# Two of three score steps between the halves of a slot's projections, and the low queries' step last

## The reference

```
Q = query @ w_q.T;  K = ctx @ w_k.T;  V = ctx @ w_v.T        # split into 16 heads
scores = einsum('bhqd,bhkd->bhqk', Q, K) / sqrt(32)
attn = softmax(scores);  c = einsum('bhqk,bhkd->bhqd', attn, V)
z = c @ w_o.T + b_o + query
out = (z - mean(z)) * rsqrt(var(z) + eps) * gamma + beta
```

## Time and profile before

| | us |
|---|---|
| median of 3 runs | 531.98 (531.88 to 532.25) |
| the profiled execution | 532.36 |
| its span, first to last instruction | 530.4 |
| mean granted TensorE clock | 0.995 |

### The profile page before, as it was taken

The page is one execution under the profiler, slowest core; times in us unless marked ns, Lnnn a source line. Parts: engine busy times, 40 slices in busy tenths (PEclk is TensorE's granted clock), DMA queues, the critical chain, the costliest instruction groups (busy, mean ns, idle before and its releaser), DMA issues.

```text
span 530.4 us, 12625 instructions
## 1 busy us (share of the span) xinstructions
PE 520.6 (98%) x4522; PEld 373.1 (70%) x4522; DVE 425.5 (80%) x877; ACT 423.9 (80%) x794; POOL 447.5 (84%) x387
## 2 busy tenths in 40 slices
PE   8999999999999999999999999999999999999994
PEld 7765577777777777777777767777766777777563
DVE  7886768887887778787878887888788778877887
ACT  6657777888888888888888888888888888877783
POOL 1725867999999999999999999999999999977956
PEclk9999999999999999999999999999999999999998
DMA  8953422344334332443243324333433432222123
GB/s 291 272 147 97 122 85 84 106 125 125 90 112 131 126 104 93 133 130 104 86 134 121 110 92 130 109 117 103 126 100 108 125 126 64 74 75 87 44 83 120
DMA packets 56750, 61.12 MB, mean 115 GB/s; under 512 B 29168, under 2 KB 29168, under 8 KB 56688
## 3 DMA queue, kind: packets, MB, share of 16 engines
q1 hardware_dynamic: 56688, 60.32, 36.4%
HBM read 39.58 MB, written 16.78 MB: 106 GB/s over the span
## 4 chain that ended last, share of the span: by engine, by line
PE 94%; DVE 3%; ACT 2%; issue 1%; DMA 0%; SPq 0%; DVEq 0%
PE ps_q L440 53%; PE ps_s L399 12%; PE ps_s L372 8%; PE ps_o L446 6%; PE ps_q L299 5%; PE ps_s L383 3%; PE ps_o L299 3%; PE ps_s L299 2%; PE ps_s L306 1%; DVE stats L812 1%; DVE z L808 1%; DMA max_rows<-max_turned 0%; ACT inverse L572 0%; DVE y L826 0%; DVE q_lo L722 0%
## 5 line engine op out<-in xcount | busy, mean ns | idle before, releaser
L446 PE MATMUL ps_o<-wo_hi,c_lo 64*128 64x512 f32 x448 | 180.1, 402 | 0.0
L440 PE MATMUL ps_q<-x_hi,wq_lo 64*128 64x512 f32 x448 | 179.8, 401 | 0.2 <-issue 0.2
L446 PE MATMUL ps_o<-wo_hi,c_hi 64*128 64x512 f32 x448 | 173.7, 388 | 0.0
L440 PE MATMUL ps_q<-x_hi,wq_hi 64*128 64x512 f32 x448 | 173.7, 388 | 0.0
L446 PE MATMUL ps_o<-wo_lo,c_hi 64*128 64x512 f32 x448 | 173.4, 387 | 0.0
L440 PE MATMUL ps_q<-x_lo,wq_hi 64*128 64x512 f32 x448 | 173.2, 387 | 0.0
L440 PEld LDWEIGHTS ps_q<-x_hi,wq_lo 64*128 64x128 f32 x448 | 82.4, 184 | 58.0 <-DVE z L808 46.1
L945 POOL TENSOR_TENSOR c_lo<-c_raw,c_hi 128x512 fp32r<-128x512 f32 x63 | 81.8, 1298 | 41.7 <-ACT c_hi L529 41.7
L969 POOL TENSOR_TENSOR y<-y,beta_row 128x512 f32<-128x512 f32 x59 | 103.9, 1760 | 4.6
L440 PEld LDWEIGHTS ps_q<-x_hi,wq_hi 64*128 64x128 f32 x448 | 82.4, 184 | 14.9
L440 PEld LDWEIGHTS ps_q<-x_lo,wq_hi 64*128 64x128 f32 x448 | 82.7, 185 | 12.6
(11 more groups left out here) (111 smaller groups left out, 1085.5 us busy)
## 6 DMA issues: line engine op xcount, KB each, us to landing
xT_raw<-in_xT SPq DMA_DIRECT2D x64, 256.0 KB, 3.0
x_raw<-in_x SPq DMA_DIRECT2D x64, 256.0 KB, 2.8
out<-y SPq DMA_DIRECT2D x64, 256.0 KB, 2.0
max_rows<-max_turned SPq DMA_DIRECT2D x128, 16.0 KB
ctx_raw<-in_ctxT SPq DMA_DIRECT2D x4, 256.0 KB, 5.1
wk_raw<-in_wkT SPq DMA_DIRECT2D x4, 256.0 KB, 5.3
wq_raw<-in_wqT SPq DMA_DIRECT2D x4, 256.0 KB, 6.0
wv_raw<-in_wvT SPq DMA_DIRECT2D x4, 256.0 KB, 6.7
```

The costliest lines, as they stand in the source:

```text
L440: return nc.tensor.matmul(ps_q[:, 0, :], w[l][half, k, dims], x_[r][half, qc % 2, k, :], start=(half is lower and k == 0 and step == 0), s ...
L446: return nc.tensor.matmul(ps_o[:, 0, :], cx[l][half, k, tile], wo[r][half, k, :], start=(half is upper and k == 0 and step == 0), stop=(ha ...
```

## The change

Of the three steps of a slot's scores, steps 0 and 1 now stand between the halves of `project_both` in the loop, and step 2 alone behind the second half; before it was step 0 between and steps 1 and 2 behind. The table of passes has its last two entries swapped, for every call of `score`: step 1 is now high keys by high queries, and step 2 high keys by low queries. The waits ahead of step 0 are as they were.

```diff
@@ -364,7 +364,7 @@
                     wait(pe, c_raw_done, n - 2)
-                passes = ((kbd_lo, q_hi), (kbd_hi, q_lo), (kbd_hi, q_hi))
+                passes = ((kbd_lo, q_hi), (kbd_hi, q_hi), (kbd_hi, q_lo))
                 for step in steps:
                     lhs, rhs = passes[step]
                     for pair in range(2):
@@ -494,9 +494,9 @@
             for t in range(OUT_LAG, SLOTS - 1):
                 project_both(t + 1, t - OUT_LAG, False)
                 subtract_max(t - 2)
-                score(t, range(1))
+                score(t, range(2))
                 project_both(t + 1, t - OUT_LAG, True)
-                score(t, range(1, 3))
+                score(t, range(2, 3))
                 combine_values(t - 2)
```

## The result

The changed kernel takes 538.5 us in the median against 532.04 for the one before, a ratio of 1.0118 (95% interval 1.0107 to 1.013): 6.5 us slower, where no change was forecast. Its profiled execution took 537.88 us with a span of 535.9, 5.5 us over the one before in both. The clock is no part of it, 0.996 against 0.995.

The account below looks back on a forecast made before the run. The prediction took TensorE's own steps, 7.62 us per slot over 56 slots, to bound the kernel. All terms were 0, so the 531.98 us median gave a forecast of 532.0 us, no change, with a range of 530.9 to 533.5.

Parts of the forecast that it names:

- The bound: Loop slot: 7.62 us as a sum of TensorE's own steps, none held by another engine.
- the 0.84 in front of L440: Slot start: the weight load's listed wait for z is the time of combine_values itself, 0.84 each, 46.1 us in total.
- Rival 3: Start of each slot: z or q_raw arrives after combine_values, TensorE stands; up to 12.7 us, 544.7; chance 0.03.
- The moved step: Between the halves: a score step costs 0.23 there as at the end; 0, bounded at 0.6 us either way.
- the swapped order: Score passes: kbd_hi x q_lo last releases nothing, since score() still waits for q_lo_done ahead of step 0; 0.
- Rival 1: Seams between the halves settle differently: +1.3 us (533.3), chance 0.08, or -1.2 us (530.8), chance 0.09.
- ACT: Query copies and q_hi shift 0.23 into 0.24 of idle time; log_sums slips 0 to 0.02; 0, bounded at 1.1 us.
- Rival 2: ACT's slip reaches c_raw once q_hi ends later than 0.22 into the slot: 2.2 us, 534.2; chance 0.04.
- DVE is the step that failed: DVE's z and q_lo move about 0.21 later; the shift vanishes in 0.97 of idle time in front of divide; 0.
- 0.77 of idle time: Sign in the changed trace: DVE's wait ahead of divide falls from 0.97 to about 0.77.
- the 2.83 that the prediction named as a sign of being wrong: c_raw should end 2.77 to 2.79 into the slot; the prediction is wrong if it ends after 2.83.
- The sentence on POOL: POOL's work hangs on c_hi, x_hi and y of ACT, behind log_sums, and does not move; cost 0.

Follow-up runs that it names:

- the collision is away: Changed kernel with POOL waiting for q_lo of the same slot before it adds beta, so that DVE goes first: 532.9 us, ratio 1.0011.
- nudged: Kernel before, scores as they were, with one tiny 128x8 memset on DVE in front of q_lo in each slot: 537.11 us, ratio 1.0092.
- all-in-the-middle kernel: Kernel before with all three score steps between the halves, none behind the second half, without POOL's wait for q_lo: 544.34 us, ratio 1.0236.

## Why the prediction was wrong, point by point

**The bound** was read rightly: the slot is a sum of TensorE's steps, and the 0.84 in front of L440 is no wait for z. It is 46.1 us in 55 pieces in the changed kernel too, with z 0.34 later in the slot. Rival 3 did not come about.

**The moved step** at 0, bounded at 0.6 us, and **the swapped order** at 0 held: 0.69 for three steps in the middle once the collision is away, with 0.6 us left over, and 0.9999 for the order alone. Rival 1 isn't needed for the loss; its count was off, though: nine slots of the kernel before take 7.65 or more, not about a dozen.

**ACT** held to a hundredth: log_sums slipped from 0.18 to 0.21, where 0.02 was the bound, and c_raw to 2.79 where nothing else was late. Rival 2 named the gate and nearly its place (2.83; it is 2.85), but put only ACT in front of it.

**DVE is the step that failed**: "q_lo, which moves from 265.26-265.91 to about 265.47-266.12 ... The 0.21 vanishes there." The start was right to 0.02, 0.67 in the slot. The duration was not; I had carried over the 0.65 as if it belonged to the instruction. It was 1.67, and where I had 0.77 of idle time left in front of divide, c_raw ended at 2.94, 0.17 late and past the 2.83 that the prediction named as a sign of being wrong. The term that I had at 0 is 55 x 0.10 = 5.5 us, and the remaining 0.01 per slot is within the slots' own variation.

The profile before had it in three places. POOL's addition of beta had a mean of 1760 ns where the multiplication by gamma, the same form, had 1302: it was waiting for something half a microsecond in each slot, with no row in the table of waits. Behind the slot of rows 3, the addition started at 265.26, the very start of q_lo in rows 6 (POOL's timeline):

```profile
263.89 1.29 POOL L967 TENSOR_TENSOR y<-y,gamma_row 128x512 f32<-128x512 f32 x1
265.26 1.82 POOL L969 TENSOR_TENSOR y<-y,beta_row 128x512 f32<-128x512 f32 x1
```

And one slot of the kernel before had already gone the other way (timelines of POOL and DVE):

```profile
295.73 1.29 POOL L969 TENSOR_TENSOR y<-y,beta_row 128x512 f32<-128x512 f32 x1
...
295.77 1.79 DVE L722 TENSOR_TENSOR q_lo<-q_raw,q_hi 128x512 fp32r<-128x512 f32 x1
...
297.49 0.68 DVE L798 TENSOR_TENSOR c_raw<-ps_s,inverse 128x512 f32<-128x512 f32 x1
```

c_raw ended at 2.84 there, still in time, so the slot itself gave no sign. I had moved q_lo by 0.21 past POOL without asking what POOL was doing there. The sentence on POOL, that its work "does not move", was nearly true (the addition of beta starts at 0.50 in the slot instead of 0.44) and missed the point: it was the neighbour that stood still.

The Trainium skill, in its page SBUF — State Buffer, section Who interferes with whom, states the rule: a DVE instruction with two inputs in SBUF contends with a GpSimd instruction that reads SBUF, not with one that only writes; the port that they share is an exclusive lock, and issue order decides who blocks. This case's traces agree: q_lo takes 1.42 to 1.82 with a reading neighbour ahead of it, and 0.65 beside a writing one as it does alone, and who waits changed with an order shifted by a few hundredths. In the changed, the nudged and the all-in-the-middle kernel q_lo starts at 0.67, 0.52 and 0.89 in the slot, and every long one ends 0.55 after POOL's addition does, as if it got nowhere while that lasts. c_raw, with one input in PSUM, is not slowed by POOL's addition of the bias that runs beside it (0.68).

Settled are the collision, the gate and their share of the loss. Left open are the last 0.6 us, whether it is POOL's reading or its computing that holds DVE up (the page says reading), and why a few slots in each trace show a pause of 0.28 to 0.37 on ACT or DVE, with the neighbour named as releaser or none.

## What to carry to other kernels

Before moving an instruction on one engine, look at what runs beside it on the other engines, at the old time and at the new one; a duration read off one timeline holds only with those neighbours. An instruction that takes longer at one line than the same form does at another (1760 ns against 1302 here) may be waiting for something that no table of waits lists. And where two such instructions start within hundredths of each other, fix their order with a semaphore so that the one with slack waits: here it cost nothing (0.9998), and it brought the cost of this shift from 6.5 us down to 0.6.

## What the runs showed of the hardware

- DVE's subtraction of two 128x512 SBUF tiles takes 0.65 us alone. Behind the start of a POOL addition of 1.30 that reads SBUF it takes 1.42 to 1.82 and ends 0.55 after the addition; POOL's takes 1.82 behind DVE's. Neither stretch appears as idle time: both count as busy.
- A POOL memset of 128x512, 0.53 us, does not slow the same subtraction down.
- Two instructions that meet like this can change places when one of them moves by less than 0.1 us; recorded starts that lie within 0.04 of each other don't say which of them waits.
- A group of 64-row matmuls that waits for the end of another on TensorE itself started without delay with two steps of 0.23 us between them; with one, its first step was 0.10 longer, by the releaser that the trace names.
